# Three of 64 gathered columns replaced by bilinear sums over the whole image on TensorE

## The reference

```
wi = conv3x3(x, w_offset) + b_offset            # 27 values per pixel
o1, o2, m = split(wi, 3); mask = sigmoid(m)     # for 9 taps: y offset, x offset, mask
py, px = o1 + base_y, o2 + base_x               # where each tap reads
y0, x0 = floor(py), floor(px); dy, dx = py - y0, px - x0
sampled = (v00*(1-dy)*(1-dx) + v01*(1-dy)*dx + v10*dy*(1-dx) + v11*dy*dx) * mask
out = einsum('bkcp,fck->bfp', sampled, filt)    # 9 taps x 64 channels -> 64 filters
x = x + out
```

## Time and profile before

| | |
|---|---|
| time, median of 3 runs | 796.09 us (794.35 to 797.31) |
| profiled execution | its span, from the first to the last instruction, is 791.9 us; its own device time was not recorded apart, and the median above is 4.2 us longer than the span |
| busy, share of the span | PE 85%, PEld 75%, DVE 67%, ACT 31%, POOL 70% |
| chain that ended last | POOL 42%, PE 24%, issue 17%, DVE 14% |

### The profile page before, as it was taken

One profiled execution on the slowest core, in us unless ns is written; L12 is line 12 of the kernel. 1 busy time (PEld: TensorE's weight loads), 2 busy tenths in 40 slices (PEclk: granted clock), 3 DMA queues, 4 the chain that ended last, 5 costly groups with the idle time before them and its releaser, 6 DMA issues.

```text
span 791.9 us, 14534 instructions
## 1 busy us (share of the span) xinstructions
PE 675.1 (85%) x4714; PEld 596.5 (75%) x4714; DVE 533.5 (67%) x901; ACT 242.8 (31%) x471; POOL 550.6 (70%) x589
## 2 busy tenths in 40 slices
PE   8998888899899989998798989988798987564665
PEld 6877668798788888888777877878788977454555
DVE  4785578777977897788667796678667885222122
ACT  4514421543154214522254214412254213000000
POOL 2203777777777777777777777777777777777774
PEclk9999889999999999999899998999899998555557
DMA  5103333533453435343454335343354335433332
GB/s 168 57 4 98 107 110 108 161 110 110 115 161 112 123 109 165 108 128 108 115 157 129 108 114 159 114 122 107 112 162 114 109 112 161 116 109 113 107 109 73
DMA packets 55139, 92.75 MB, mean 117 GB/s; under 512 B 13384, under 2 KB 35480, under 8 KB 55064
## 3 DMA queue, kind: packets, MB, share of 16 engines
q0 software_dynamic: 27264, 74.49, 32.4%
q1 hardware_dynamic: 27064, 16.93, 7.7%
q10 hardware_dynamic: 736, 0.41, 0.2%
HBM read 79.37 MB, written 12.40 MB: 116 GB/s over the span
## 4 chain that ended last, share of the span: by engine, by line
POOL 42%; PE 24%; issue 17%; DVE 14%; ACT 2%; DMA 1%; POOLq 0%; DVEq 0%; SPq 0%; ACTq 0%
POOL pixels L606 42%; PE banks L1247 16%; PE banks L1250 8%; DVE weighted L984 3%; DVE prod L892 1%; DVE prod L874 1%; DVE banks L835 1%; DVE prod L880 1%; DVE prod L855 1%; DMA pixels<-table,index 1%; DVE prod L854 1%; DVE row_squares L622 1%; ACT coef_T L1136 0%; DVE xn L666 0%; DVE xc L650 0%
## 5 line engine op out<-in xcount | busy, mean ns | idle before, releaser
L606 POOL DMA_INDIRECT pixels<-table,index x568 | 540.1, 951 | 204.2 <-issue 172.2
L1250 PE MATMUL banks<-const,weighted 128*128 128x128 f32 x1280 | 193.6, 307 | 54.9 <-DVE weighted L984 44.6
L984 DVE TENSOR_TENSOR weighted<-pixels,banks 128x2304 f32<-128x2304 f32 (+1 forms) x65 | 161.1, 2479 | 116.3 <-DMA pixels<-table,index 112.6
L1250 PEld LDWEIGHTS banks<-const,weighted 128*128 128x128 f32 x1280 | 168.5, 163 | 65.8 <-DVE weighted L984 48.8
L1148 ACT ACTIVATE sampled_T<-banks 128x512 f32<-128x512 f32 (+1 forms) x128 | 55.8, 436 | 327.5 <-PE banks L1250 327.5
L1250 PE MATMUL banks<-const,prod 128*128 128x128 f32 x816 | 110.3, 278 | 14.1 <-DVE prod L854 7.3
L1250 PEld LDWEIGHTS banks<-const,prod 128*128 128x128 f32 x816 | 90.9, 143 | 22.8 <-DVE banks L836 8.6
L1247 PE MATMUL banks<-conv_w,xT 128*128 128x64 f32 (+2 forms) x576 | 97.7, 325 | 0.7 <-ACT banks L1125 0.7
L1247 PEld LDWEIGHTS banks<-conv_w,xT 128*128 128x128 f32 x576 | 91.4, 191 | 7.0 <-ACT banks L1125 1.6
L1247 PE MATMUL banks<-filt,sampled_T 128*128 128x64 f32 x640 | 88.0, 288 | 7.2 <-ACT sampled_T L1148 7.2
L1247 PEld LDWEIGHTS banks<-filt,sampled_T 128*128 128x128 f32 x640 | 82.5, 204 | 13.6 <-ACT sampled_T L1148 11.5
(11 more groups left out here) (159 smaller groups left out, 675.9 us busy)
## 6 DMA issues: line engine op xcount, KB each, us to landing
far_pixels<-table SPq DMA_DIRECT2D x1024, 1.0 KB
pixels<-table,index POOLq DMA_INDIRECT x568, 2.7
table<-xn SPq DMA_DIRECT2D x46, 128.0 KB
table<-xn SPq DMA_DIRECT2D x16, 144.0 KB
x<-x_in SPq DMA_DIRECT2D x30, 64.0 KB, 2.4
out_dram<-x SPq DMA_DIRECT2D x60, 32.0 KB
table<-corner_w SPq DMA_DIRECT2D x16, 70.0 KB
const<-const_in SPq DMA_DIRECT2D x2, 384.0 KB, 4.5
```

The lines of the kernel that those rows point to most:

```text
L606: pool.indirect_dma_start(out=pixels[:, col % NB, k, :], out_offset=None, in_=table[0:(u + 1) * TY * TX, :], in_offset=bass.IndirectOffset ...
L984: return dve.tensor_tensor(weighted[:, col % 2, :, a:b, :].rearrange("p q k c -> p k q c"), entries.rearrange("p k (q c) -> p k q c", c=C) ...
L1250: return pe.matmul(dst, data, moved, start=start, stop=stop, is_transpose=True, skip_group_check=True)
```

## The change

The last three columns (w = 5, 6, 7 of each side) of the eighth image are no longer gathered. So 61 columns are gathered instead of 64, with 541 gathers instead of 568; the tap that SP fetches for the eighth image is now one of column 60. For each of the three, numbered d = 0, 1, 2, the kernel forms for every tap and target pixel the sum over all 1024 source pixels of source times weight, where the weight is bilinear in the distance from the tap's position. The source pixels lie on the 128 partitions (row and side) and on 8 columns within a partition, so it is 8 passes, one for each column w', and one more that lets the weight be written with a minimum:

sum v * hat_y * (1 - min(|dx|, 1)) = sum over (v summed over w') * hat_y, minus the sum over w' of v * hat_y * min(|dx|, 1)

The new pieces:

- `wneg`, `wsum`: the negated sources (ACT) and their sum over w' (DVE).
- `ws0` to `ws5` (PE): 23 transposes a column that throw y, x and mask of all targets over all partitions, into one PSUM bank, four at a time; `wt0` to `wt5` (ACT) takes each four out, the y values as a distance.
- `why` (ACT): hat of y, 1152 elements a partition; `wy` (DVE): copies it to PSUM.
- `wdx0` to `wdx7` (ACT): |x - position of w'|, 1152 elements; `ww0` to `ww7` (DVE): times hat of y, 1024 + 128 elements; a ring of 3 buffers.
- `wp0` to `wp8` (PE): the nine passes. The stationary operand is the source, 128 partitions x 64 channels; the moving one the weights of four taps (512 columns, to PSUM partitions 0 to 63), of four more (512 columns, to partitions 64 to 127) and of the ninth (128 columns).
- `wT` (DVE): times mask; `wf` (PE): filter; after the third, `wadd` (DVE) adds all three to `x`. Then SP stores them, four transfers, and only then the last gathered column.

The buffers are those of the first layer, which is over. PSUM banks 3 and 2 take the sums, bank 5 the thrown values.

```diff
+WIDE = 3
+LAST = B * WS - 1 - WIDE
+WIDE_W = WS - WIDE
+WIDE_PASSES = WS + 1
...
-                for w in range(WS):
+                for w in range(WIDE_W if u == UNITS - 1 else WS):
...
+            sp.wait_ge(s_wide_x2, 1)
+            store_sides(sp, UNITS - 1, WIDE_W, WIDE, range(SIDES))
+            sp.wait_ge(s_x2, UNITS * GROUPS_U + (LAST % COLS > 0))
+            store_sides(sp, UNITS - 1, (GROUPS_U - 1) * COLS, COLS - WIDE, (0, 1))
...
+            def weights_of_pass(d, w):
+                n = d * WIDE_PASSES + w + 1
+                dst, far = wide_w[n % WIDE_RING], far_x[(d * WS + w) % WIDE_RING]
+                if n >= WIDE_RING:
+                    dve.wait_ge(s_pass, n - WIDE_RING + 1)
+                dve.wait_ge(s_ramp, d * WS + w + 1)
+                dve.wait_ge(s_hat_ps, 2 * (d + 1))
+                dve.scalar_tensor_tensor(dst[:, 0:2 * HALF], far[:, 0:2 * HALF], 1.0, hat_y, ALU.min, ALU.mult)
+                dve.scalar_tensor_tensor(dst[:, 2 * HALF:], far[:, 2 * HALF:], 1.0, hat_y_last, ALU.min, ALU.mult)\
+                   .then_inc(s_wide_w, 1)
...
+            def masked_sums(d):
+                dst, by = wide_T[d % 2], wide_mask[d % 2]
+                dve.wait_ge(s_pass, (d + 1) * WIDE_PASSES)
...
+                dve.tensor_tensor(dst[:, 0:HALF], wide_sums, by[:, 0:HALF], ALU.mult)
+                dve.tensor_tensor(dst[0:C, HALF:], last_sums, by[0:C, HALF:], ALU.mult).then_inc(s_wide_T, 1)
...
+            def distances_x(d, w):
+                n = d * WS + w
+                act.wait_ge(s_taken, SPREADS * d + 5)
+                if n >= WIDE_RING:
+                    act.wait_ge(s_wide_w, n - WIDE_RING + 1)
+                act.activation(far_x[n % WIDE_RING], at_x[d % 2], ACT.Abs, bias=to_right(w), scale=-1.0).then_inc(s_ramp, 1)
...
+            def sum_pass(d, i):
...
+                data, by = (summed if first else negated[:, (i - 1) * C:i * C]), wide_w[n % WIDE_RING]
+                mm(wide_sums[0:C, :], data, by[:, 0:HALF], first, last)
+                mm(wide_sums[C:P, :], data, by[:, HALF:2 * HALF], first, last)
+                mm(last_sums, data, by[:, 2 * HALF:], first, last).then_inc(s_pass, 1)
```

More of the change, by code:

```diff
@@ L100 @@
[L100 to L104, removed]
@@ L150 @@
[L150 to L154, removed]
@@ L155 @@
[L155 to L169, removed]
@@ L1148, in copy_part, with negated_sources, wide_masks, take @@
                 act.activation(sampled_T[:, col % 2, a * P:b * P], turned[:, 0:(b - a) * P], ACT.Copy).then_inc(s_sT, 1)
+            def negated_sources():
+                act.activation(negated, xn2_own(), ACT.Copy, scale=-1.0).then_inc(s_negated, 1)
+            def wide_masks(d):
+                at = (WIDE_W + d) * K2
+                act.wait_ge(*emptied(UNITS - 1, "off"))
+                if d >= 2:
+                    act.wait_ge(s_wide_T, d - 1)
+                act.activation(wide_mask[d % 2][:, 0:HALF].rearrange("p (k c) -> p k c", c=C),
+                               mask[:, at:at + K2 - 1].unsqueeze(2).to_broadcast([P, K2 - 1, C]), ACT.Copy).then_inc(s_widened, 1)
+            def take(d, i):
+                act.wait_ge(s_spread, SPREADS * d + i + 1)
+                first, last = 4 * i, min(4 * i + 4, VALUES)
+                for dst, a, b in ((far_y, 0, K2), (at_x[d % 2], K2, 2 * K2), (wide_mask[d % 2], 2 * K2, VALUES)):
+                    at, to = max(a, first), min(b, last)
+                    if at >= to:
+                        continue
+                    here, there = dst[:, (at - a) * P:(to - a) * P], thrown[:, (at - first) * P:(to - first) * P]
+                    if a:
+                        ins = act.activation(here, there, ACT.Copy)
+                    else:
+                        ins = act.activation(here, there, ACT.Abs, bias=to_below(), scale=-1.0)
+                ins.then_inc(s_taken, 1)
+            def hats_y(d):
+                n = d * WIDE_PASSES
+                act.wait_ge(s_taken, SPREADS * d + 3)
+                if n >= WIDE_RING:
+                    act.wait_ge(s_pass, n - WIDE_RING + 1)
+                act.activation(wide_w[n % WIDE_RING], far_y, ACT.Relu, bias=one, scale=-1.0).then_inc(s_hat_y, 1)
+            def distances_x(d, w):
+                n = d * WS + w
+                act.wait_ge(s_taken, SPREADS * d + 5)
+                if n >= WIDE_RING:
+                    act.wait_ge(s_wide_w, n - WIDE_RING + 1)
+                act.activation(far_x[n % WIDE_RING], at_x[d % 2], ACT.Abs, bias=to_right(w), scale=-1.0).then_inc(s_ramp, 1)
             for i in (2, 3):
@@ L1522, in filtered, with spread_values @@
                 ins.then_inc(s_out, 1)
+            def spread_values(d, i):
+                u, w = UNITS - 1, WIDE_W + d
+                n = SPREADS * d + i
+                if n:
+                    pe.wait_ge(s_taken, n)
+                else:
+                    pe.wait_ge(s_index, u + 2)
+                    for what in ("tR", "tL", "tF", "tC"):
+                        pe.wait_ge(*emptied(u, what))
+                for j in range(4 * i, min(4 * i + 4, VALUES)):
+                    of, k = divmod(j, K2)
+                    if of < 2:
+                        at = (2 * w + of) * K2 + TAP_ORDER[k]
+                        values = pos[:, at:at + 1].to_broadcast([P, P])
+                    elif k < TAP_PAIRS - 1:
+                        pe.wait_ge(s_widened, d + 1)
+                        values = pair(wide_mask[d % 2], k)
+                    else:
+                        at = w * K2 + K2 - 1
+                        values = mask[:, at:at + 1].to_broadcast([P, P])
+                    ins = flip(pair(thrown, j - 4 * i), values, eye, j == 4 * i)
+                ins.then_inc(s_spread, 1)
@@ L1615, in _ @@
                     filtered(n)
+                elif name[:-1] == "ws":
+                    spread_values(n, int(name[-1]))
+                elif name[:-1] == "wp":
+                    sum_pass(n, int(name[-1]))
+                elif name == "wf":
+                    filter_wide(n)
 def constants():
```

255 lines of the change are left out of this document (195 added, 60 removed).

## The result

The changed kernel takes 773.28 us (median of 4 runs, 772.15 to 775.08), the kernel before 795.35 us beside it (794.35 to 797.31). The ratio is 0.9727, 95% interval 0.971 to 0.9744: faster by 22 us. Predicted were 779.5 us and 774 to 793: the kernel is faster by the mechanism that was forecast, but the forecast time is 6.2 us too high, and the measured one lies 0.7 us under the range. The profiled execution took 774.22 us, with a span of 772.0.

What follows compares the result with a forecast made beforehand. POOL's gathers were taken as the bound. Last gather at 747.94, last add at 769.2, plus 2.45 and 1.7 gave span 773.3; 2 for clock and 4.2 outside the span gave 779.5 us, range 774 to 793.

Steps and rivals of the forecast that it cites:

- the 4.2 us that were set between the profiled span and the time of a run: Outside the span: profiled span 4.2 us under the median of runs, added to span 775.3 to give time 779.5.
- the 2.0 us for a lower clock: PE behind the last gather: at a granted clock of 0.87 its 15 us there take 2 us more.
- The mechanism: POOL: dropping 27 gathers gains 33.75 us, of which about 17 is given back behind the last gather.
- the sum of the end: Behind the last gather: last add at 769.2, then 2.45 and 1.7 us to the span's end at 773.3.
- 27 gathers at 1.25 us, all ahead of the end: POOL: 33.75 us removed, so the last gather starts at 747.94 instead of 781.69.
- wait of the ring: Rival, buffers tying ACT, DVE and PE: late weighings hold POOL up, 5 us at most, time 784; chance 0.06.
- DVE and ACT hide: Up to the last gather's landing: DVE's 52 us and ACT's under 50 fit under the gathers, in 79 us.
- The pass, 1.25 us side by side: PE: a pass's two 512-column matmuls overlap on different array halves, 1.25 us a pass; chance 0.47.
- In sequence: Rival on PE: a pass's matmuls run one behind another, 2.2 us a pass, time 784 to 792; chance 0.28.
- The end behind the last gather: From the last gather's start to the last add: 21 us, where it was 7.8.
- The case that I feared, half clock through all the new work: Rival on PE: clock stays low, at half clock time 830 or 881; clock too low has chance 0.14.
- 0.15 us a pass: PE: switching between whole and partial array, about 0.1 us each, 42 switches for 27 passes.

Runs made afterwards that it cites:

- e8_after_again: The changed kernel itself, unedited, run once more beside the later follow-up kernels: 774.16 us, ratio 0.974 to the kernel before.
- e1_one_half: The changed kernel with each pass's second 512-column matmul writing to PSUM partitions 0 to 63 like the first: 782.68 us, ratio 0.9849 to the kernel before.
- e6_light_dve: The changed kernel without the 1024-element weight operation on DVE in the third wide column: 774.34 us, ratio 0.9747 to the kernel before.
- e4_busy: The kernel before with three unneeded 512-column matmuls behind the filter of each column from 52 on: 794.79 us, ratio 1.0.
- e5_four: The changed kernel with four wide columns, finished as early as they fit, and last stores split between SP and ACT: 760.94 us, ratio 0.9591 to the kernel before.

## Why the prediction was right, and where it was wrong

Two steps failed, and both were added behind the sum of the work: the 4.2 us that were set between the profiled span and the time of a run, where 2.2 were measured, and the 2.0 us for a lower clock, where the profiled execution shows none in that end. The mechanism and the sum of the end held.

- **27 gathers at 1.25 us, all ahead of the end.** Right. The last gather starts at 746.77 in the profile and at 747.92 in that of `e8_after_again`; forecast 747.94. No wait of the ring reached POOL behind 672 us.
- **DVE and ACT hide.** Right. `ww` took 1.21 + 0.28 us at 1.33 us from one to the next (forecast 1.53 each), ACT's 1152 elements 1.25 (forecast 1.13), DVE was busy 51 us from 672 to 752 (forecast 52).
- **The pass, 1.25 us side by side.** Right: 1.08 in a row, 1.2 to 1.3 alone. The choice that carried most of the doubt, at little more than even odds, is settled by `e1_one_half`. In sequence it is 1.93, not 2.2, since my 0.95 ns a column was too high: a record of 512 columns advances PE by 0.43 us, 0.84 ns a column, in `e4_busy` (six in 2.79 us, of which the last takes 0.64).
- **The end behind the last gather.** Right in size, 21.1 us to the end of the last add for 21.3 and stores of 4.14 for 4.15, but in part by luck. The nine passes took some 10.1 us on PE instead of 11.25 (an estimate from the steps above). Against that PE waited 1.57 us for ACT's copy, which stands in ACT's list behind a distance that itself waited 1.49 us for a buffer of the ring, and 0.5 for DVE's last weights, where 0.75 in all had been set. That DVE and PE end at about the same time was right: `e6_light_dve` puts half a microsecond between them.
- **The clock term, 2.0 us.** Not there in the profiled execution: PE ran at 1.00 from 740 to 760, and its last filter took 1.33 us, as in the kernel before at 651.26, where the granted clock was 1.00 (646 to 653). In `e8_after_again` the clock from 740 to 760 was 0.91: it was 0.53 from 744 to 746 and 0.61 from 746 to 748, after PE had been busy 1.1 of the 4 us before, and 1.00 from there to the last add. From the last gather to the end of the last add it was 21.8 us, 0.7 more. The case that I feared, half clock through all the new work, did not come: 0.98 from 672 to 752, and 0.96 in `e8_after_again`.
- **The 4.2 us outside the span.** Wrong, and the plainest error. I took the difference between one span and the median of other executions for a fixed cost. In the eight executions of the changed kernel the difference between time and span is 2.2 to 2.3 us, in the 20 of the kernel before that have both numbers 2.1 to 2.2, and in all the others 1.8 to 2.3 (the 1.8 to 2.0 in `e5_four` alone, whose last stores are split). By these the profiled execution of before took about 794.1 us, 2.0 under the median that I used. It was a short one, which says nothing about the changed kernel.

So 6.2 us of error are 2.0 of the clock, 2.0 outside the span, and 2.2 between my span of 773.3 and the median span of the runs, 771.1. The last is no step that failed: eight executions of the changed kernel have spans from 769.7 to 773.8. In the profiled one, 772.0, 1.2 us of the difference stand ahead of the last gather.

That the two matmuls of 512 would run side by side was my choice in the prediction, from their sharing no column of the array and no output; no row of the kernel before shows it. The runs agree with it: 1.08 against 1.93 us a pass. For the change between the whole array and a part of it the prediction set 0.15 us a pass, an estimate from the earlier trace rows. The trace fits: a pass between other work keeps PE 1.22 us (754.60 to the filter at 755.82) where one in a row keeps it 1.08. No run shows that these 0.14 us are the cost of that change.

## What to carry to other kernels

When work is moved off the engine that bounds the kernel onto idle ones, its gain is what the bound loses minus what is ordered behind the bound's last piece: list first what stands there, and move it ahead. The same instructions gave 22 us in one order and 34 in the other, and 34 was all that the 27 gathers held. Where the stationary operand has 64 columns, it is worth trying to put two matmuls on the two halves of the array, with their sums in the two halves of the PSUM partitions: here it took 0.85 us from a pass of 1.93, and without it the better order gains nothing that can be told.

## What the runs showed of the hardware that was not expected

Part of the difference between single profiles arises in the first ten microseconds, where all these kernels do the same work. PE's rows at 5 us and the first gather, of `e8_after_again` and then of `e5_four`:

```profile
5.62 3.76 PE L1412 MATMUL banks<-x,ones 128*128 128x512 f32 x4
...
70.00 1.12 POOL L665 DMA_INDIRECT pixels<-table,index  x1 [31.41 <-DMA table<-xn]
```

```profile
5.42 1.96 PE L1416 MATMUL banks<-x,ones 128*128 128x512 f32 x4
...
67.51 1.12 POOL L667 DMA_INDIRECT pixels<-table,index  x1 [31.39 <-DMA table<-xn]
```

The same four records took twice as long in the one, and the first gather came 2.5 us later. It looks like half the clock, but the granted clock of the profile is 1.00 from 5 to 10 us in both, so the cause is open. Of ten profiles, three have 1.96 us there, and in them the first gather starts at 67.5; seven have 3.7 to 3.8, and it starts at 69.4 to 70.0. No kernel was profiled in both ways, and what decides in which way an execution begins was not tried. A difference of 2 us between two single profiles of these kernels may be just this.
